# Expert rows added to a buffer in memory by accumulating scatters, and copied from there to the output

## The reference

```python
x = x + _L0_xattn_ref(_layernorm(x), ctx_1024, ctx_1024, ...)
# mixture of experts, 8 experts, the best 2 for each token:
probs = softmax(dot(xn, router_w))
expert_gate, expert_index = top_k(probs, 2)
v = selected_matmul(xb, wv, sv)           # xb: each token twice
y = gelu(selected_matmul(xb, w, s))
out = selected_matmul(v * y, w1, s1)      # 4096 rows of 128
x = x + sum over the 2 experts of expert_gate * out
```

## Time and profile before

| | us |
|---|---|
| median of 3 runs | 297.25 (297.24 to 297.35) |
| span of the profiled execution | 280.1 |
| median less span (what lies around the span) | 17.15 |
| PE busy | 240.8 |
| DVE busy | 189.6 |
| POOL busy | 169.6 |
| ACT busy | 113.7 |

### The profile page before, as it was taken

The page is one execution under the profiler, slowest core; times in us unless marked ns, Lnnn a source line. Parts: engine busy times, 40 slices in busy tenths (PEclk is TensorE's granted clock), DMA queues, the critical chain, the costliest instruction groups (busy, mean ns, idle before and its releaser), DMA issues.

```text
span 280.1 us, 5789 instructions
## 1 busy us (share of the span) xinstructions
PE 240.8 (86%) x1587; PEld 216.4 (77%) x1588; DVE 189.6 (68%) x461; ACT 113.7 (41%) x281; POOL 169.6 (61%) x155
## 2 busy tenths in 40 slices
PE   7999788888888898996559998999999999999800
PEld 7988566667766677774348998999999999999700
DVE  3777999998976877966974567554545555555416
ACT  2414322344433442314145944555555555555100
POOL 7949659899858888699804777744242424242410
PEclk9979799999889959997555999999999999999975
DMA  4969991000000010000112123331111121100059
GB/s 145 305 136 417 305 366 60 1 0 0 0 4 19 10 34 16 0 20 1 50 41 65 48 78 106 102 94 46 42 50 50 35 56 37 38 10 28 7 173 276
DMA packets 22506, 22.90 MB, mean 82 GB/s; under 512 B 2716, under 2 KB 17984, under 8 KB 22354
## 3 DMA queue, kind: packets, MB, share of 16 engines
q1 hardware_dynamic: 18700, 17.30, 20.8%
q0 software_dynamic: 2528, 4.77, 5.3%
q10 hardware_dynamic: 1254, 0.55, 0.7%
HBM read 16.26 MB, written 6.80 MB: 82 GB/s over the span
## 4 chain that ended last, share of the span: by engine, by line
PE 70%; POOL 11%; issue 6%; ACT 4%; DMA 4%; DVE 3%; SPq 1%; POOLq 0%; ACTq 0%; DVEq 0%
PE bank L884 26%; PE bank L801 14%; PE bank L901 12%; POOL sums_in L326 6%; POOL routed L537 3%; PE bank L726 3%; PE bank L798 2%; DMA sums_in<-expert_out 2%; PE bank L820 2%; PE bank L871 2%; PE bank L822 2%; PE bank L821 2%; PE bank L789 1%; ACT xn L590 1%; PE bank L781 1%
## 5 line engine op out<-in xcount | busy, mean ns | idle before, releaser
L326 POOL TENSOR_TENSOR sums_in<-sums_in,ctx_ig 128x2048 f32<-128x2048 f32 x15 | 67.6, 4510 | 9.4 <-ACT sums_in L598 9.3
L551 POOL DMA_INDIRECT expert_out<-yo,xs x39 | 37.9, 972 | 56.2 <-DVE yo L1224 54.3
L801 PE MATMUL bank<-qk,ident 128*128 128x256 f32 x256 | 63.1, 403 | 0.0
L801 PEld LDWEIGHTS bank<-qk,ident 128*128 128x128 f32 x256 | 53.0, 207 | 8.6
L1007 DVE TENSOR_REDUCE bank<-sums_in 128x144 f32<-128x2304 f32 x16 | 40.9, 2556 | 9.3 <-POOL sums_in L326 9.3
L884 PE MATMUL bank<-xsT,g_tile 128*128 128x128 f32 x312 | 42.4, 280 | 1.1 <-issue 1.1
L537 POOL DMA_INDIRECT routed<-rows,pos x32 | 33.1, 1035 | 15.8 <-issue 15.5
L884 PE MATMUL bank<-xsT,v_tile 128*128 128x128 f32 x312 | 42.1, 279 | 0.0
L901 PE MATMUL bank<-w_sb,ctx_sb 128*128 x312 | 41.4, 276 | 0.0
L884 PEld LDWEIGHTS bank<-xsT,g_tile 128*128 128x128 f32 x312 | 38.9, 196 | 1.3 <-issue 1.3
L1214 DVE TENSOR_TENSOR ctx_sb<-bank,ctx_sb 128x512 f32<-128x512 f32 x39 | 26.9, 691 | 19.1 <-PE bank L884 16.7
(11 more groups left out here) (167 smaller groups left out, 305.1 us busy)
## 6 DMA issues: line engine op xcount, KB each, us to landing
xs<-routed SPq DMA_DIRECT2D x39, 65.0 KB, 1.9
g_sb<-in_L_ffn_w_dram SPq DMA_DIRECT2D x1, 2048.0 KB, 9.9
g_scale<-in_L_ffn_s_dram SPq DMA_DIRECT2D x1, 2048.0 KB, 14.7
v_sb<-in_L_ffn_wv_dram SPq DMA_DIRECT2D x1, 2048.0 KB, 24.8
sums_in<-expert_out SPq DMA_DIRECT2D x3, 512.0 KB, 4.8
x_sb<-in_x_dram SPq DMA_DIRECT2D x4, 256.0 KB, 6.1
ctx_sb<-in_ctx_dram SPq DMA_DIRECT2D x4, 256.0 KB, 6.9
out_dram<-x_sb SPq DMA_DIRECT2D x3, 256.0 KB, 2.9
```

Of the source, the lines that this page charges most:

```text
L326: return eng.tensor_tensor(pv[:, b, :, :].rearrange("p (h i) g -> p h i g", h=H), probs[:, b, :, :].unsqueeze(2).to_broadcast([P, H, HD, H ...
L551: pool.indirect_dma_start(out=expert_out[:, :], out_offset=bass.IndirectOffsetOnAxis(ap=xs_i[:, t % XB, P:P + 1], axis=0), in_=yo[:, t % X ...
L801: mm = nc.tensor.matmul(bank[2 + b][:, 0:H * H], ident[:, :], qk[:, b, i, :], start=False, stop=(i == HD - 1))
```

## The change

The buffer in memory is now `summed`, 2048 rows and 128 more for pads. SP writes the residual rows to it, one transfer for each group of four tiles (`residual`, semaphore `preset`). Both rows of a token go to the token's own row, and the scatter adds to what lies there (`compute_op=ALU.add`). The pads have the 128 rows behind the tokens' as destinations, and are written. The first scatter waits for all four preset transfers, and each other one until the scatter before it has landed. At the end SP and ACT each wait until all scatters have landed, and each copies half of `summed` to the output, as 128 pieces of 4 KB. The loads of pairs, DVE's additions and the chunked stores are gone.

```diff
--- before.py
+++ after.py
@@ -43,7 +43,6 @@
 EARLY = -(-(TOP * TOKENS * EARLY_G // NG - E * (P - 1)) // P)
 LEFT = TILES - EARLY
 ROWS = E * REGION + SPARE * P
-NOWHERE = 1 << 20
 XB = 12
 EPS = 1e-5
 SCALE = DK ** -0.5
@@ -80,7 +79,7 @@
         group_sum, slot, place = in_bank7(E), in_bank7(G, E), in_bank7(TOP, G)
 
         routed = nc.dram_tensor("routed", [ROWS, ROWW], F32, kind="Internal").ap()
-        expert_out = nc.dram_tensor("expert_out", [TOP * TOKENS, P], F32, kind="Internal").ap()
+        summed = nc.dram_tensor("summed", [TOKENS + P, P], F32, kind="Internal").ap()
 
 
         ident = sb("ident", [P, P])
@@ -199,11 +198,6 @@
         hid = ctx_flat[:, 2 * F:4 * F].rearrange("p (b n) -> p b n", b=2)
         xs_i = xs[:, :, :].bitcast(I32)
 
-        got = [sums_in[:, g // 2, (g % 2) * (P // 2):(g % 2 + 1) * (P // 2), :].rearrange("p m g -> p (m g)")
-               for g in range(NG)]
-        fin = qk[:, :, :, :].rearrange("p a (q i) s -> p (a q) (i s)", q=2)
-
-
         ld_small, ld_wo, ld_bo, ld_router, ld_sv = (sem(n) for n in (
             "ld_small", "ld_wo", "ld_bo", "ld_router", "ld_sv"))
         ld_x = [sem(f"ld_x{g}") for g in range(NG)]
@@ -246,9 +240,8 @@
         g_tile_ready, v_tile_ready = sem("g_tile_ready"), sem("v_tile_ready")
         act_ready, hid_ready, y_psum, yo_ready = (sem(n) for n in ("act_ready", "hid_ready", "y_psum", "yo_ready"))
 
-        CHUNKS = [(0, 4), (4, 4), (8, 4), (12, 3), (15, 1)]
-        got_rows = [sem(f"got_rows{n}") for n in range(len(CHUNKS))]
-        pair_sum, fin_ready, stored = sem("pair_sum"), sem("fin_ready"), sem("stored")
+        preset, stored = sem("preset"), sem("stored")
+        HALF = TOKENS // 2
 
         POOL_SET, EPS_SET = 17, 8
         SHARE = E * FC // (G * (NG - 2))
@@ -316,10 +309,6 @@
                     step(g, j)
             for j in range(AHEAD):
                 step(NG - 1, j)
-
-        def got_of(t0, many):
-
-            return got[t0 // G][:, t0 % G * TOP * P:(t0 % G + many) * TOP * P].rearrange("p (t n) -> p t n", t=many)
 
         def values(eng, t, b):
 
@@ -357,6 +346,18 @@
 
             return i + (c // XB + 1)
 
+
+        def copy_out(eng, half):
+
+            at = slice(half * HALF, (half + 1) * HALF)
+            rows = HALF // P
+            return eng.dma_start(out.rearrange("t p d -> (t p) d")[at, :].rearrange("(a r) d -> a (r d)", r=rows),
+                                 summed[at, :].rearrange("(a r) d -> a (r d)", r=rows))
+
+        def all_added(eng):
+
+            for b in range(XB):
+                eng.wait_ge(y_sent[b], 16 * len(range(b, TILES, XB)))
 
         twice = lambda w: w.unsqueeze(1).to_broadcast([w.shape[0], 2, DK])
         SMALL = ((q9[0:HD, :], Wq), (k9[0:HD, :], Wk), (q9[HD:HD + 1, :], bq.unsqueeze(0)),
@@ -393,10 +394,22 @@
                     r0 = sp.value_load(row_off[0:1, bass.ds(i * XB + c, 1)], min_val=0, max_val=ROWS - P)
                     sp.dma_start(xs[:, c, :], routed[bass.ds(r0, P), :]).then_inc(xs_loaded[c], 16)
 
+                def residual(g):
+
+                    sp.wait_ge(x2_ready, g * G + G)
+                    sp.dma_start(summed[g * G * P:(g + 1) * G * P, :].rearrange("(t p) d -> p t d", p=P),
+                                 x_sb[:, at[g], :]).then_inc(preset, 16)
+
+                for g in range(EARLY_G):
+                    residual(g)
                 sp.wait_ge(early_ready, 1)
                 sp.wait_ge(scattered, SENT * (EARLY_G + 1))
                 for c in range(EARLY):
                     load(0, c)
+
+
+                for g in range(EARLY_G, NG):
+                    residual(g)
 
                 sp.wait_ge(pads_known, 1)
                 for e in range(E):
@@ -415,20 +428,13 @@
                     load(whole, c)
 
 
-                for b in range(XB):
-                    sp.wait_ge(y_sent[b], 16 * len(range(b, TILES, XB)))
-                pairs = expert_out.rearrange("(t p k) d -> p t (k d)", p=P, k=TOP)
-                out_rows = out.rearrange("t p d -> p t d")
-                for n, (t0, many) in enumerate(CHUNKS):
-                    sp.dma_start(got_of(t0, many), pairs[:, t0:t0 + many, :]).then_inc(got_rows[n], 16)
-                for n, (t0, many) in enumerate(CHUNKS):
-                    sp.wait_ge(fin_ready, n + 1)
-                    sp.dma_start(out_rows[:, t0:t0 + many, :], x_sb[:, t0:t0 + many, :]).then_inc(stored, 16)
-                sp.wait_ge(stored, 16 * len(CHUNKS))
+                all_added(sp)
+                copy_out(sp, 0).then_inc(stored, 16)
+                sp.wait_ge(stored, 16 * 2)
 
             @block.gpsimd
             def _(pool):
-                last_row, last_dest = pool.to_reg(ROWS - 1), pool.to_reg(TOP * TOKENS - 1)
+                last_row, last_dest = pool.to_reg(ROWS - 1), pool.to_reg(TOKENS + P - 1)
                 steps = [0]
 
                 def built(ins):
@@ -455,14 +461,14 @@
                                 allow_small_or_imprecise_dtypes=True))
                 built(pool.iota(region0[:, :, :], pattern=[[0, G], [REGION, E]], base=0, channel_multiplier=0,
                                 allow_small_or_imprecise_dtypes=True))
-                built(pool.iota(dest[:, :, :], pattern=[[TOP * P, NT], [1, TOP]], base=0, channel_multiplier=TOP,
+                built(pool.iota(dest[:, :, :], pattern=[[P, NT], [0, TOP]], base=0, channel_multiplier=1,
                                 allow_small_or_imprecise_dtypes=True))
                 built(pool.iota(tile_edges[:, :, :], pattern=[[0, E], [P, NT]], base=0, channel_multiplier=0,
                                 allow_small_or_imprecise_dtypes=True))
                 built(pool.iota(tile_no[:, :, :], pattern=[[1, TILES], [0, E]], base=0, channel_multiplier=0,
                                 allow_small_or_imprecise_dtypes=True))
                 built(pool.memset(pad_rows[:, :], 0.0))
-                built(pool.iota(pad_rows[:, P:P + 1].bitcast(I32), pattern=[[0, 1]], base=NOWHERE, channel_multiplier=0))
+                built(pool.iota(pad_rows[:, P:P + 1].bitcast(I32), pattern=[[0, 1]], base=TOKENS, channel_multiplier=1))
                 assert steps[0] == POOL_SET
 
 
@@ -548,11 +554,15 @@
 
                 for t in range(TILES):
                     pool.wait_ge(yo_ready, t + 1)
+                    if t == 0:
+                        pool.wait_ge(preset, 16 * NG)
+                    else:
+                        pool.wait_ge(y_sent[(t - 1) % XB], 16 * ((t - 1) // XB + 1))
                     pool.indirect_dma_start(
-                        out=expert_out[:, :],
+                        out=summed[:, :],
                         out_offset=bass.IndirectOffsetOnAxis(ap=xs_i[:, t % XB, P:P + 1], axis=0),
                         in_=yo[:, t % XB, :], in_offset=None,
-                        bounds_check=last_dest, oob_is_err=False).then_inc(y_sent[t % XB], 16)
+                        bounds_check=last_dest, compute_op=ALU.add).then_inc(y_sent[t % XB], 16)
 
             @block.scalar
             def _(act):
@@ -714,6 +724,8 @@
                 ffn(0, 2)
                 ffn(0, 3)
                 ffn_steps(act, ffn)
+                all_added(act)
+                copy_out(act, 1).then_inc(stored, 16)
 
             @block.tensor
             def _(pe):
@@ -1253,17 +1265,6 @@
                 ffn_steps(dve, ffn)
 
 
-                for n, (t0, many) in enumerate(CHUNKS):
-                    dve.wait_ge(got_rows[n], 16)
-                    two = got_of(t0, many).rearrange("p t (k d) -> p t k d", k=TOP)
-                    first = t0 % G * P
-                    part = fin[:, t0 // G, first:first + many * P].rearrange("p (t d) -> p t d", t=many)
-                    v.tensor_tensor(part, two[:, :, 0, :], two[:, :, 1, :], ALU.add).then_inc(pair_sum, 1)
-                    dve.wait_ge(pair_sum, n + 1)
-                    at = x_sb[:, t0:t0 + many, :]
-                    v.tensor_tensor(at, at, part, ALU.add).then_inc(fin_ready, 1)
-
-
 # ---- launch: one core; inputs and outputs as the reference has them ----
 _INS = ['x', 'ctx_1024', 'L0_xattn_Wq', 'L0_xattn_bq', 'L0_xattn_Wk', 'L0_xattn_bk', 'L0_xattn_Wv', 'L0_xattn_bv',
         'L0_xattn_Wo', 'L0_xattn_bo', 'L0_ffn_router_w', 'L0_ffn_wv', 'L0_ffn_sv', 'L0_ffn_w', 'L0_ffn_s',
```

## The result

The changed kernel takes 343.09 us (median of 4 runs, 342.18 to 343.84) against 297.3 for the kernel before: a ratio of 1.149 (95% interval 1.144 to 1.155), 46 us slower. The forecast was 320 us, with a range of 297 to 352. The sign and the mechanism are as forecast, the size is not: 22.7 us more were forecast, 45.8 came.

The account below looks back on a forecast made before the run. PE bounds most of the span (70% of the chain), then a 12.2 us tail. Chained scatters at 3.18 us a link land last at 296.8; plus 5.8 of tail and 17.15 around the span gives 319.7, say 320 us (297 to 352).

Parts of the forecast that it names:

- The tail: Behind the last landing: two copies replace loads, additions and stores, 5.8 us in place of 12.2, 6.4 us less.
- The chain isn't hidden: Scatters on POOL: each waits for the landing before, links of 3.18 us, last landing at 296.8, 28.9 us later.
- Rival 1: Scatter chain: waits are hidden, adding is free, landings stay at 2.1 us; 292.0 us, chance 0.12.
- The gap between landing and issue: On POOL, from a scatter's landing to the next issue: 0.3 us in each link.
- What adding costs: In each scatter's landing: adding takes 0.4 us more, so a landing of 2.88 us.
- The third side on POOL: POOL's issue of an adding scatter: a third side, the read of 128 rows, costs 0.27 to 0.49 us.
- the forecast's own case: Scatter chain: adding costs 0.1 to 1.2 us a landing, chance 0.62.
- The start: First scatter on POOL, right behind the last of routing: starts at 173.07 us as in the kernel before.
- What lies around the span: Outside the profiled span: 17.15 us (297.25 less 280.1), added to the forecast span of 302.6.
- PE starves late, at no cost: Late loads wait for slots as the chain runs up to 28 us behind; PE waits, costing nothing of its own.
- Rivals 3 and 4: At each scatter, reads in series with the write, 371 us, chance 0.08; at the end, copies of 8.2 us, not 5.3.

Follow-up runs that it names:

- experiment 4: Kernel before with only its end changed: two copies of the first 2048 expert rows replace loads, additions and stores; 290.56 us (0.976).
- experiment 7: Changed kernel with the output itself as the buffer scatters add to, pads skipped, end copies gone, chain kept; 340.08 us (1.143).
- experiment 2: Changed kernel with plain scatters in place of adding ones, chain of waits kept; 305.53 us (1.023).
- experiment 3: Changed kernel with adding scatters but no waits between them, each expert row having a row of its own; 292.35 us (0.982).
- experiment 5: Changed kernel with the two waits ahead of each scatter swapped, landing of the scatter before first; 325.7 us (1.097).
- experiment 1: Kernel before, unchanged, run again for a second profile; 297.22 us, span of 295.2 us.
- experiment 10: Changed kernel again, beside a kernel before of 283.04 us: 338.99 us (1.195); with the waits swapped 323.09 us (1.141).
- experiment 6: Changed kernel with plain scatters and the two waits swapped; 289.79 us beside a kernel before of 282.97 (1.026).

## Why the prediction was right in kind and short in size

The forecast's own steps, in the trace's time:

- **The tail.** 5.8 us forecast, 6.1 measured; the copies took 5.5 for 5.3. Right. The saving that experiment 4 finds is real (7.1 us). That experiment 7 finds little more when the copies go is due to POOL's drain, which no step of the forecast had.
- **The chain isn't hidden.** Right: experiments 2 and 3 show it from both sides. Rival 1's time, 292 us, came true only where the waits were gone (292.35), and not for the changed kernel, whose shortest landing was 3.2.
- **The gap between landing and issue.** 0.3 us was taken from the rows of scatters that waited for DVE or nothing. It was 0.74. This step failed: the row was of one wait, that goes with the instruction, and the change has two. 38 x 0.44 is 16.7 us; experiment 5 gets 17.4 back.
- **What adding costs.** 0.4 us taken, 0.91 measured against plain scatters in the same chain (experiment 2), the mean landing 3.35 in place of 2.88: 39 x 0.47 is 18.3 us. The third side on POOL was put at 0.27 to 0.49 and is 0.58. The rest, 0.33, is in the transfer, where 0.1 was put for the read. The direction of both parts was right, the sizes weren't. The 0.91 lies inside the forecast's own case, adding at 0.1 to 1.2 us.
- **The start.** 176.45 in place of 173.07, 3.4 us. The 8 late routing scatters, ahead on POOL, waited for ACT. This is no price of the change: the second profile of the kernel before starts at 176.26 too (experiment 1), and beside a kernel before of 283 us the changed kernel starts at 174.1.

Together 16.7 + 18.3 + 3.4 are 38.4 us, and 0.3 of tail: span 302.6 + 38.7 = 341.3, as measured.

- **What lies around the span.** 17.15 us were added to the span. This step failed, by 15.3 us the other way (1.8 measured), and so the errors partly hid each other: 319.7 + 38.7 - 15.3 = 343.1. That the forecast is 23 us off and not 38.7 is luck. The 15.3 us were no surroundings but what ordinary executions had and the profiled one lacked (experiment 1): a stall of 12.1 us in the chain of waits, and ahead of it a later start, 3.2 us by the first scatter. A chain that starts on POOL, which doesn't stall, and is slower than PE in any case absorbs the stall, though not the later start (experiment 10). So the forecast made the changed kernel pay for a stall that it hides.
- **PE starves late, at no cost.** Right. PE idles before line 883 for loads (15.1 us in 16 waits), and SP's 30 late loads, which took 62.7 us to issue, take 100.4. PE's last products end before 300 us, 35 us before the last landing.
- **Rivals 3 and 4.** Adding at 1.9 us didn't come true (0.91), nor slow end copies.

The Trainium skill's rule on accumulating transfers ("DMA: Bandwidth & Descriptors", Rules for kernel authors) made the wait necessary; adding without it over shared rows wasn't tried, so no run here shows the lost additions that the rule is about. The Trainium skill's factor for an add with two reads ("Collectives: The Full Stack", Why ReduceScatter is half of AllGather) is two, for the bandwidth of a collective; here a link's landing grew from 2.44 to 3.35 us, by 1.37, and the 1 MB transfer took 7.8 us where copies took 5.5, by 1.42, though that is one queue beside two. The Trainium skill's fit ("DMA: Bandwidth & Descriptors", Anatomy of one DMA), 2.15 us for 64 KB, is near the shortest plain landing (2.1), lies under the mean that a chain pays (2.44 to 2.57) and doesn't hold for one that adds (3.2 at the least).

## What to carry to other kernels

When a change turns independent transfers into a chain, multiply the link (mean landing, not median, plus the gap behind a landing) by their number, and ask how much slack is in the whole row and not in one tile. An addition in a transfer cost next to nothing here where nobody waited for its landing (1.8 us in all) and 0.91 us each time where the next transfer did. If a profile's span and the median of the runs don't fit, find out what the profiled execution lacks before you add the difference as a constant.

## What the runs showed of the hardware that was not expected

- A scatter of 128 rows of 512 B that adds takes POOL 1.55 us to issue in place of 0.97, and lands after 3.3 us in place of 2.3.
- After a landing awaited by an instruction of its own, 0.74 us pass until POOL issues; awaited by the scatter itself, 0.27.
- POOL's drain at the end of the program lasts 6.5 us beyond its last scatter instruction (340.4 less 333.8; the same in experiments 2, 3 and 6).
- Wherever the kernel before took 297 us, each trace but its first has a wait of ACT's of 10 to 13 us near 170 us that the profile doesn't explain, in which DVE and PE stop too and POOL doesn't; where it took 283 us, none of the four traces has it. The same chip showed both (297.6 and 283.0 us). What ACT waits for is not settled.
